# Loads on two queues, a permuted token dimension and a reordered first chunk in a gated-delta and ternary-FFN kernel

## What is computed

```python
def gated_delta(x, Wq, Wk, Wv, Wo, Wb, bb, Wd, bd):
    q, k, v = x @ Wq, x @ Wk, x @ Wv
    beta, delta = sigmoid(x @ Wb + bb), softplus(x @ Wd + bd)
    # per step t:  S = beta[t][:, None] * S + delta[t][:, None] * outer(k[t], v[t]);  o[t] = q[t] @ S
    return o @ Wo

def ffn(x, w1, w2, w3):     # quantize(w) = clip(round(w / (mean|w| + 1e-8)), -1, 1)
    return (sigmoid(x @ quantize(w1).T) * (x @ quantize(w2).T)) @ quantize(w3).T

x = x + gated_delta(layernorm(x), ...)
x = x + ffn(layernorm(x), w1, w2, w3)
```

## Time and profile before

| | us |
|---|---|
| median of 3 runs | 328.5 (328.18 to 328.82) |
| the profiled execution | 328.81 |
| its span, first to last instruction | 327.1 |
| PE busy | 319.8 |
| DVE busy | 210.1 |
| ACT busy | 142.4 |
| POOL busy | 107.4 |

### The profile page before, as it was taken

The page is one execution under the profiler, slowest core; times in us unless marked ns, Lnnn a source line. Parts: engine busy times, 40 slices in busy tenths (PEclk is TensorE's granted clock), DMA queues, the critical chain, the costliest instruction groups (busy, mean ns, idle before and its releaser), DMA issues.

```text
span 327.1 us, 5876 instructions
## 1 busy us (share of the span) xinstructions
PE 319.8 (98%) x2152; PEld 176.1 (54%) x2152; DVE 210.1 (64%) x474; ACT 142.4 (44%) x281; POOL 107.4 (33%) x339
## 2 busy tenths in 40 slices
PE   7999999999999999999999999999999999999996
PEld 5888779874445444445454444454544444444445
DVE  6789899899998767366688543666886312433311
ACT  3687896789855571323143260231431102232200
POOL 7298325599913016980030136500201100000000
PEclk9999999999999999999999999999999999999999
DMA  6999900647841625300003051000030720000011
GB/s 180 382 388 395 360 4 0 104 91 133 125 85 32 114 49 81 113 0 2 0 2 64 2 129 61 7 2 0 2 64 0 93 102 1 0 2 0 0 66 64
DMA packets 45805, 26.99 MB, mean 83 GB/s; under 512 B 37584, under 2 KB 38352, under 8 KB 45776
## 3 DMA queue, kind: packets, MB, share of 16 engines
q1 hardware_dynamic: 45456, 26.62, 31.0%
q10 hardware_dynamic: 320, 0.00, 0.0%
HBM read 13.89 MB, written 4.19 MB: 55 GB/s over the span
## 4 chain that ended last, share of the span: by engine, by line
PE 78%; DVE 10%; DMA 3%; SPq 3%; ACT 2%; issue 2%; DVEq 0%; ACTq 0%
PE ffn L1199 40%; PE ffn L1217 23%; PE lev L1120 4%; DMA x_sb<-in_L_attn_x_dram 3%; PE ffn L1044 3%; DVE w_nat L841 2%; DVE X L854 2%; SPq L282 2%; PE lev L1077 2%; PE pd L1054 2%; PE oc L1104 1%; DVE abs_part L821 1%; DVE w_nat L848 1%; DVE xnT L989 1%; DVE sc L881 1%
## 5 line engine op out<-in xcount | busy, mean ns | idle before, releaser
L1199 PE MATMUL ffn<-w_nat,w12T 128*128 128x512 f16 x704 | 155.4, 379 | 0.6 <-DVE xnT L989 0.6
L1199 PEld LDWEIGHTS ffn<-w_nat,w12T 128*128 128x128 f16 x704 | 67.8, 98 | 83.0 <-issue 3.7
L1217 PE MATMUL ffn<-w3T,w_nat 128*128 128x512 f16 (+1 forms) x374 | 76.7, 366 | 0.0
L718 ACT ACTIVATE xnT<-ffn 128x512 f32<-128x512 f32 x44 | 26.1, 593 | 97.5 <-PE ffn L1199 97.5
L989 DVE SCALAR_TENSOR_TENSOR xnT<-ffn,xnT 128x512 f32<-128x512 f32 x44 | 30.2, 687 | 52.3 <-PE ffn L1199 51.9
L1217 PEld LDWEIGHTS ffn<-w3T,w_nat 128*128 128x128 f16 x374 | 36.6, 98 | 40.7 <-ACT w_nat L724 1.0
L402 POOL TENSOR_TENSOR ve<-mv,rconst 128x2 f32<-128x2 f32 x12 | 2.5, 210 | 118.1 <-DVE mv L758 118.1
L1005 DVE SCALAR_TENSOR_TENSOR x_sb<-ffn,x_sb 128x512 f32<-128x512 f32 (+1 forms) x17 | 11.2, 659 | 42.8 <-PE ffn L1217 42.8
L994 DVE TENSOR_TENSOR w_nat<-xnT,w_nat 128x512 f16<-128x512 f32 x44 | 32.2, 732 | 0.4
L724 ACT ACTIVATE w_nat<-xnT 128x512 f16<-128x512 f32 x44 | 27.4, 623 | 8.4 <-DVE xnT L989 8.3
L881 DVE COPY_PREDICATED sc<-mask,lev 128x128 f32<-128x128 uint32 x56 | 18.9, 338 | 2.9 <-PE oc L1091 1.3
(11 more groups left out here) (142 smaller groups left out, 368.2 us busy)
## 6 DMA issues: line engine op xcount, KB each, us to landing
x_sb<-in_L_attn_x_dram SPq DMA_DIRECT2D x16, 256.0 KB, 8.4
out_dram<-x_sb SPq DMA_DIRECT2D x15, 256.0 KB, 2.0
w_nat<-in_L_ffn_w_dram SPq DMA_DIRECT2D x2, 1536.0 KB, 12.2
w_nat<-in_L_ffn_w_dram SPq DMA_DIRECT2D x2, 1408.0 KB, 14.7
w_nat<-in_L_ffn_w_dram SPq DMA_DIRECT2D x2, 1280.0 KB, 12.9
wv<-in_L_attn_Wv_dram SPq DMA_DIRECT2D x1, 256.0 KB, 5.8
wo<-in_L_attn_Wo_dram SPq DMA_DIRECT2D x1, 256.0 KB, 13.5
out_dram<-x_sb SPq DMA_DIRECT2D x2, 128.0 KB, 1.7
```

The costliest lines, as they stand in the source:

```text
L718: nc.scalar.activation(sig[:, u % 2, :], bank[2 * u % 3][:, :], ACT.Sigmoid, scale=1.0 / XS).then_inc(sig_ready, 1)
L1199: done = nc.tensor.matmul(bank[n % 3][:, :], w12T[:, a * DT + t, u * P:(u + 1) * P], xT[:, g, part, t, :], start=t == 0 and part == 0, sto ...
L1217: done = nc.tensor.matmul(bank[(2 * HT + m + h) % 3][:, cols], hid[:, part, j, m * P:(m + 1) * P], w3T[:, j, cols], start=part == 0 and j ...
```

## The change

- The loads. SP: x(0), Wv, x(1), Wb and Wd, x(2), x(3), the two bd, w1's first half, x(4), w1's second half, and on as before. x(4) thus goes ahead of one FFN half of 1280 KB. ACT issues the two bb and then Wq and Wk. The projection weights lie with four consecutive rows to a partition: partition p holds rows 4p to 4p+3, and block t is row 4p+t.
- To match, the normalised token is written permuted: block t of `xn` takes elements t, 4+t, 8+t, ... of the 512, so the normalising instruction reads f32 at a step of four elements (16 bytes) and writes contiguously. That is so in `quick_apply` (DVE, six times), `apply` on ACT (five times) and `apply` on DVE (five times). The transposes and projections are the same instructions; only which of the 512 stands where is changed.
- PE: v(0,0) runs ahead of z(0) in the place of keep_warm(6); T(1,0) runs between z(0)'s `wqk` and `wbd` halves; T(1,1) follows z(0), then v(0,1) and z(1). `weights_in` becomes `wqk_in` and `wbd_in`.
- ACT: the copy of T(1,0) goes ahead of zcopy(0); that of T(1,1) stays behind it.

```diff
             load_x(0)
-            for dst, w in ((wqk[:, :, 0:K], Wq), (wqk[:, :, K:2 * K], Wk), (wbd[:, :, 0:K], Wb),
-                           (wbd[:, :, K:2 * K], Wd)):
-                sp_.dma_start(dst, w.rearrange("(t p) k -> p t k", p=P)).then_inc(weights_in, 16)
+            sp_.dma_start(wv[:, :, :], Wv.rearrange("(p t) k -> p t k", t=DT)).then_inc(wv_in, 16)
             load_x(1)
+            for dst, w in ((wbd[:, :, 0:K], Wb), (wbd[:, :, K:2 * K], Wd)):
+                sp_.dma_start(dst, w.rearrange("(p t) k -> p t k", t=DT)).then_inc(wbd_in, 16)
             load_x(2)
-            sp_.dma_start(wv[:, :, :], Wv.rearrange("(t p) k -> p t k", p=P)).then_inc(wv_in, 16)
             load_x(3)
+            for b in range(B):
+                sp_.dma_start(bias[half(b), 1:2], bd.rearrange("(k o) -> k o", o=1)).then_inc(bias_in, 16)
             load_w(0, 0)
+            load_x(4)
             load_w(0, 1)
-            load_x(4)
             load_w(1, 0)
...
                 nc.scalar.dma_start(bias[half(b), 0:1], bb.rearrange("(k o) -> k o", o=1)).then_inc(bias_in, 16)
-                nc.scalar.dma_start(bias[half(b), 1:2], bd.rearrange("(k o) -> k o", o=1)).then_inc(bias_in, 16)
+            for dst, w in ((wqk[:, :, 0:K], Wq), (wqk[:, :, K:2 * K], Wk)):
+                nc.scalar.dma_start(dst, w.rearrange("(p t) k -> p t k", t=DT)).then_inc(wqk_in, 16)
...
+        def spaced(ap):
+            return ap.rearrange("p (n t) -> p t n", t=DT)
...
-                nc.scalar.activation(xn[:, c % 2, 0, :], tile(c, 0), ACT.Identity, scale=rs[:, c, 0:1],
+                nc.scalar.activation(tiles(xn[:, c % 2, 0, :]), spaced(tile(c, 0)), ACT.Identity, scale=rs[:, c, 0:1],
                                      bias=shift[:, c:c + 1]).then_inc(xn0_ready, 1)
...
-                    nc.vector.tensor_scalar(xn[:, c % 2, b, :], tile(c, b), mv[:, c, b, 0:1], rs[:, c, b:b + 1],
-                                            ALU.subtract, ALU.mult).then_inc((xn0_ready, xn1_ready)[b], 1)
+                    nc.vector.tensor_scalar(tiles(xn[:, c % 2, b, :]), spaced(tile(c, b)), mv[:, c, b, 0:1],
+                                            rs[:, c, b:b + 1], ALU.subtract, ALU.mult).then_inc((xn0_ready, xn1_ready)[b], 1)
...
             guess(1)
+            evacuate_first(1)
             zcopy(0)
...
                 for a, w in enumerate((wqk, wbd)):
+                    if c == 0:
+                        pe.wait_ge((wqk_in, wbd_in)[a], 32)
+                        if a == 1:
+                            transposes(1, 0)
...
             transposes(0, 1)
-            keep_warm(6)
-            pe.wait_ge(weights_in, 16 * 4)
+            pe.wait_ge(wv_in, 16)
+            pe.wait_ge(xnT0_ready, 1)
+            project_v(0, (0,))
             project_z(0)
-            pe.wait_ge(wv_in, 16)
-            project_v(0, (0,))
-            turn(1)
+            transposes(1, 1)
             project_v(0, (1,))
             project_z(1)
```

More of the change, by code:

```diff
@@ L131, in build_gated_delta_ternary_ffn @@
         w_in = [[sem(f"w{n + 1}_load{h}") for h in range(2)] for n in range(3)]
-        weights_in, wv_in, wo_in = sem("weights_in"), sem("wv_in"), sem("wo_in")
+        wqk_in, wbd_in, wv_in, wo_in = sem("wqk_in"), sem("wbd_in"), sem("wv_in"), sem("wo_in")
         bias_in = sem("bias_in")
@@ L534, in _, with evacuate_first @@
                 nc.scalar.dma_start(bias[half(b), 0:1], bb.rearrange("(k o) -> k o", o=1)).then_inc(bias_in, 16)
-                nc.scalar.dma_start(bias[half(b), 1:2], bd.rearrange("(k o) -> k o", o=1)).then_inc(bias_in, 16)
+            for dst, w in ((wqk[:, :, 0:K], Wq), (wqk[:, :, K:2 * K], Wk)):
+                nc.scalar.dma_start(dst, w.rearrange("(p t) k -> p t k", t=DT)).then_inc(wqk_in, 16)
             nc.scalar.preload_act_table_set("natural_log_exp_and_others")
-            def evacuate_T(c):
+            def evacuate_first(c):
                 act.wait_ge(tile_T, 2 * c + 1)
@@ L543, in evacuate_T @@
                                      ).then_inc(xnT0_ready, 1)
+            def evacuate_T(c):
+                if c != 1:
+                    evacuate_first(c)
                 if c == C - 1:
@@ L806, in apply @@
                     dve.wait_ge(tile_T, 2 * c - 2)
-                nc.vector.tensor_scalar(xn[:, c % 2, 1, :], tile(c, 1), mv[:, c, 1, 0:1], rs[:, c, 1:2],
-                                        ALU.subtract, ALU.mult).then_inc(xn1_ready, 1)
+                nc.vector.tensor_scalar(tiles(xn[:, c % 2, 1, :]), spaced(tile(c, 1)), mv[:, c, 1, 0:1],
+                                        rs[:, c, 1:2], ALU.subtract, ALU.mult).then_inc(xn1_ready, 1)
             def gates(c):
```

## The result

The changed kernel takes 329.81 us (median of 10 runs, 329.31 to 330.08), the kernel before 328.81 (10 runs, 327.79 to 329.32). The ratio is 1.0037, with a 95% interval of 1.0029 to 1.0045: slower by 1.2 us by the ratio and by the spans of the two profiles, by 1.0 by the medians. A measurement of this kernel can tell such a difference. TensorE's granted clock was full in every run of every version (0.999 to 1.0), so it plays no part. The forecast was 328.7, no change, from a sum of +0.24. 329.81 lies inside its range of 327.4 to 330.1, but near the price of its first rival, spaced reads that are dear.

A forecast was written before the change was run, and what follows sets the result against it. A loop between PE and ACT was taken to bound the front, ACT setting z(1). -0.05 (z(1)), -0.10 (gates(1)), +0.26 and +0.13 (spaced reads) gave +0.24 us on the 328.5 median: 328.7, range 327.4 to 330.1.

The forecast's parts named there:

- first rival: Reads at a step of four cost up to +0.44 us an instruction on both engines: +1.48, 330.0 us; chance 0.28.
- ACT sets z(1): Ahead of z(1), ACT's copies and not PE's work set its start: 15.78 against 15.83, -0.05 us.
- v(0,0) ahead of z(0): PE's front: v(0,0) replaces six warming matmuls at no direct cost, freeing 0.90 us of PE behind z(0).
- second rival: PE, not ACT, sets the pace, so v(0,0)'s 0.90 us is gained whole: 327.5 us; chance 0.18.
- x(4): Loaded ahead of w1's second half: DVE's statistics start 0.69 us sooner, but only 0.10 arrives at gates(1).
- free, with 0.35 to spare: T(1,0) inside z(0), due at 11.15, finds DVE's first batch of chunk 1 ready at 10.8.
- Spaced reads on DVE: Normalising reads at a step of four: +0.13 us each on DVE, 0.26 for the two quick_apply(0) ahead of z(0).
- Spaced reads on ACT: Normalising reads at a step of four: +0.13 us each on ACT, counted once, at apply(5) ahead of wo(1).
- apply(7) free: The spaced read in apply(7) costs nothing, as 0.17 us of idle stands before zcopy(6).
- Two queues: Wq and Wk, wanted at 9.35, issued on ACT's queue as its third and fourth DMA: nothing added.
- third rival: Loads on ACT's queue share the engines with x(0) and x(1) and delay them: 329.3 us; chance 0.06.
- in how DVE and POOL meet in the gates: Under the rival that PE sets the pace (327.5 us, chance 0.18): some luck there would do the same.

The follow-up runs named there:

- the last version: Kernel before with x(4) early, copy of T(1,1) on DVE, v(0,0) ahead of z(0), Wv ahead of Wq and Wk on SP's queue: 327.89 us, 0.9977.

## Why the prediction was right and where it was wrong

**ACT sets z(1): right, and shown from both sides.** The distance from z(0) to z(1) was forecast as 6.43 (15.78 - 9.35) and measured as 6.43; the idle of PE there as 1.1 and measured as 0.97, with the releaser that was named. The order by itself is worth nothing that can be told (1.0037 against 1.0036 without it), and taking one copy from ACT brought z(1) 0.2 to 0.6 closer. So v(0,0) ahead of z(0) was given back as a wait for ACT, and the second rival, that PE sets the pace, falls.

**x(4): right.** 0.10 us of 0.69 arrived, and the DMA wait in the chain became a wait for ACT.

**T(1,0) "free, with 0.35 to spare": wrong, and it didn't show.** The batch was to be ready at 10.8. Its instruction ended at 10.96 + 0.75 = 11.71, no sooner than before (11.70), because DVE's list takes the statistics of both batches first and the second landed late:

```profile
9.58 0.69 DVE L787 BATCH_NORM_STATS2 stats<-x_sb 128x6 f32<-128x512 f32 x1 [0.28 <-issue]
...
10.96 0.75 DVE L801 TENSOR_SCALAR xn<-x_sb,mv,rs 128x512 f32<-128x512 f32 x1
```

T(1,0) found it ready at 11.89 only because z(0) was 0.74 late; from the 9.35 of the forecast it would have been due at 11.15 and have waited. That is luck.

**Spaced reads on DVE: mis-sized for one instruction, right for the path by luck.** +0.20 in the place of +0.13 for each. But the first of the two ahead of z(0) was slow before already (0.68), and together they brought z(0) 0.24 later in the version with spaced reads alone, close to the 0.26 of the sum.

**Spaced reads on ACT: the term that was mis-sized.** It had +0.13, the price of DVE's slower rows carried over to another engine, and it is +0.52. The bound of +0.44 was also too low. It counts where the prediction put it: wo(1), which had no wait, waits 0.61 for ACT. Between levels(0) and wo(1) the lag grows by 0.65, and the last wait ahead of the FFN, that of z(7) for ACT, by 0.21 (0.99 where it was 0.78); the prediction had called apply(7) free because 0.17 of idle covered 0.13. Alone the spaced reads cost 0.8 us. The point from which they were said to decide, 0.25 us an instruction, stood for one price on both engines; measured were 0.20 on DVE and 0.52 on ACT, so the runs don't test it.

The Trainium skill (Vector Engine (DVE) Microarchitecture Reference, Measured stream behaviour on trn2) gave the prediction an estimate of 0.17 us for DVE if both ports share the columns; the trace has 0.20. Its rule, full rate only for runs of two adjacent words, agrees with the pairs (0.55); by it a step of two should be dear as well, but the trace has 0.58 for it and 0.75 for a step of four, and the measurement decides.

**Two queues: the step that failed.** "Nothing added" is where the prediction looked at the issue of Wq and Wk on ACT and not at their landing. The DMAs after (bytes, median us from issue to landing), then Wk's before, then Wk's in the last version, on one queue behind Wv:

```profile
wv<-in_L_attn_Wv_dram SPq DMA_DIRECT2D x1, 256.0 KB, 5.7
...
wqk<-in_L_attn_Wq_dram ACTq DMA_DIRECT2D x1, 128.0 KB, 6.1
wqk<-in_L_attn_Wk_dram ACTq DMA_DIRECT2D x1, 128.0 KB, 7.3
```
```profile
wqk<-in_L_attn_Wk_dram SPq DMA_DIRECT2D x1, 128.0 KB, 3.9
```
```profile
wqk<-in_L_attn_Wk_dram SPq DMA_DIRECT2D x1, 128.0 KB, 5.5
```

Issued at 2.70, Wk landed at 9.96, past the 9.35 at which it was wanted. In the kernel before it was issued at 2.18 and took 3.9 us, so it was there at about 6.1. Two things were changed at once, the queue of Wk and the place of Wv, and the versions tell them apart. With Wv next to it on the one queue Wk took 5.3 to 5.9 us (four versions) and was there at 7.6 to 8.4, in time; on ACT's queue it took 6.7 to 7.3 (four versions) and was there at 9.4 to 10.0. So Wv's place takes up the slack and the second queue makes the wait. The third rival named shared engines as its mechanism, but for x(0) and x(1) and with 0.06 of the chance. That sharing is what delays Wk fits these times; they don't show it by themselves. The loads by themselves cost 0.5 us (1.0015); what the reads leave of the loss is 0.4 to 0.7. x(1)'s first batch landed at about 8.4, where I took 8.0.

**What the sum gave and didn't.** 0.8 (reads) + 0.5 (loads) = 1.3 against 1.2 measured. Between z(1), 0.69 late, and levels(0), 0.28 late, 0.4 us came back: DVE's gates(1) and chain took 5.27 us from 24.33 on, where they took 5.63 (29.33 less 23.70). The traces show what differs at its start, first before, then after:

```profile
23.75 0.47 POOL L449 TENSOR_TENSOR own<-store 128x128 f32<-128x128 f32 x1
```
```profile
24.33 0.20 DVE L824 TENSOR_SCALAR w3T<-w3T 128x128 f32<-128x128 f32 x1
...
25.06 0.45 POOL L454 TENSOR_TENSOR own<-store 128x128 f32<-128x128 f32 x1
```

DVE's first instruction of gates(1) took 0.63 in the earlier trace rows, where POOL's 128x128 `own` ran beside it, and 0.20 after, where `own` came 0.73 later. All 13 profiles agree: one of the two short instructions of gates(1) takes 0.62 to 0.69 in the six in which `own` runs beside it, and both take 0.20 to 0.26 in the other seven, three of them with contiguous reads. So the gain doesn't need the spaced reads; it is the luck "in how DVE and POOL meet in the gates" that the prediction named under its second rival. An estimate from these numbers: without the 0.36 us the time would have been about 330.2, just outside the range.

So the time fell inside the range with the price on ACT put at a quarter of what it is and the landing of Wk left out; 0.4 us of luck worked against these two.

## What to carry to other kernels

When a step reorders one engine, look up which engine releases the instruction that is meant to start sooner: the gain goes to waste unless that one is relieved too, and here the relief alone (one copy of 0.6 us moved to an idle stretch of DVE, with x(4) early) was worth 0.8 us and the reordering nothing. Price a changed access pattern on each engine that runs it; a price from one doesn't hold for another. A load moved to a second queue loses its place ahead of others: here, with Wv's new place beside it, Wk was issued 0.5 us later and landed 3.9 us later. Write down when a load must have landed, not when it is issued.

## What the runs showed of the hardware

- A normalising instruction over 128x512 f32 with a read or write at a step of 16 bytes, or a read at 64, took ACT 0.47 to 0.52 us more and DVE 0.16 to 0.22; with a read at a step of 8 bytes, or in pairs of words at 32, at most 0.05 more on ACT and nothing on DVE. The extra of the step of 16 bytes is about 1 ns a column on ACT.
- A short DVE instruction over 128x128 f32 took 0.62 to 0.69 us where a POOL instruction of 128x128 ran beside it, and 0.20 to 0.26 where POOL ran only instructions of 128x4 or less (13 profiles).
- Wv with four rows to a partition (2 KB pieces) landed 4.9 us after its issue. With 512 bytes, in the same place of the queue, it took 5.0 to 5.8 in four profiles, so a gain isn't shown. For the loads of 64 columns the layout changed nothing (3.8 to 4.1 us against 3.4 to 4.2).
- The same load of 128 KB, Wk, landed 3.9 to 4.0 us after its issue on SP's queue with Wb and Wd behind it, 5.3 to 5.9 with Wv next to it, and 6.7 to 7.3 on ACT's queue with SP's full beside it.
